# Second attention: high and low part of the values on 128 rows, two products per batch instead of three

## The reference

```python
q = rmsnorm(hidden @ Wq.T, q_norm_w)
k = rmsnorm(repeat(ctx @ Wk.T, 4), k_norm_w)
v = repeat(ctx @ Wv.T, 4)
scores = einsum('bhqd,bhkd->bhqk', q, k) / sqrt(128) + mask
probs = softmax(scores)
x = x + einsum('bhqk,bhkd->bqhd', probs, v).reshape(...) @ Wo.T
```

## Time and profile before

| what | value |
|---|---|
| median of 3 runs | 1542.92 us (1541.38 to 1546.04) |
| the profiled execution | 1540.48 us, its span 1538.7 us |
| mean granted TensorE clock | 0.990 of full speed |
| TensorE products, busy | 1498.0 us, 97% of the span, 9676 instructions |
| VectorE, busy | 1011.8 us, 66% |
| ScalarE, busy | 819.7 us, 53% |
| GpSimd, busy | 382.1 us, 25% |
| DMA | mean 39 GB/s |
| value products of the second attention (L905) | 384 instructions, 39.64 us busy |

### The profile page before, as it was taken

How to read it: one execution, slowest core, us unless ns; L and a number is a source line. 1 busy time by engine, 2 the same in 40 slices (tenths; PEclk the granted TensorE clock), 3 DMA queues, 4 the chain that set the end, 5 groups by cost and what they waited for, 6 DMA issues and landing times.

```text
span 1538.7 us, 27892 instructions
## 1 busy us (share of the span) xinstructions
PE 1498.0 (97%) x9676; PEld 1320.9 (86%) x9676; DVE 1011.8 (66%) x2475; ACT 819.7 (53%) x2862; POOL 382.1 (25%) x390
## 2 busy tenths in 40 slices
PE   8999999999999999999999999999999999889997
PEld 8999999999989998787888888888888887777785
DVE  7566556655665567875666666566666688788775
ACT  5456455645554555446565656555556563555542
POOL 5102010201021012133232323233232331543420
PEclk9999999999999999999999999999999999989998
DMA  6000100100010101110101010101010110111001
GB/s 220 29 28 28 42 29 28 42 28 28 28 56 1 42 29 29 53 42 28 42 28 42 29 42 28 42 28 42 29 53 18 36 56 8 38 36 62 28 8 58
DMA packets 14768, 60.22 MB, mean 39 GB/s; under 512 B 2100, under 2 KB 3508, under 8 KB 9640
## 3 DMA queue, kind: packets, MB, share of 16 engines
q1 hardware_dynamic: 14632, 58.46, 10.9%
HBM read 56.36 MB, written 2.10 MB: 38 GB/s over the span
## 4 chain that ended last, share of the span: by engine, by line
PE 59%; issue 27%; DVE 7%; POOL 4%; ACT 2%; DMA 0%; POOLq 0%; DVEq 0%; ACTq 0%
PE psY L918 15%; PE psQ L837 11%; PE psKV L859 8%; PE psSO L806 3%; PE psSO L905 2%; PE psTP L869 2%; PE psQ L822 2%; PE psSO L807 2%; POOL wo L513 1%; PE psTP L822 1%; PE psTP L889 1%; PE psKV L1251 1%; PE psQ L1205 1%; PE psQ L762 1%; PE psSO L1234 1%
## 5 line engine op out<-in xcount | busy, mean ns | idle before, releaser
L918 PE MATMUL psY<-wo,oT 128*128 128x512 f32 x1536 | 384.9, 399 | 0.9 <-POOL wo L513 0.2
L918 PEld LDWEIGHTS psY<-wo,oT 128*128 128x128 f32 x1536 | 278.2, 188 | 64.9 <-POOL wo L513 2.3
L513 POOL TENSOR_TENSOR wo<-stage_o,wo 128x512 fp32r<-128x512 f32 x68 | 87.3, 1316 | 310.4 <-ACT wo L1350 310.4
L1350 ACT ACTIVATE pT<-psTP 128x512 fp32r<-128x512 f32 (+1 forms) x128 | 62.8, 491 | 162.3 <-PE psTP L889 162.3
L1442 ACT ACTIVATE prob<-wide,neg_mx 128x128 f32<-128x128 f32 x256 | 99.7, 391 | 82.1 <-DVE neg_mx L1980 82.1
L628 POOL TENSOR_TENSOR rms<-ms_eps,minus_half 128x5 f32<-128x5 f32 (+1 forms) x64 | 74.2, 1159 | 259.5 <-DVE ms_eps L1997 258.7
L1439 ACT ACTIVATE prob<-s_sb,neg_mx 128x64 f32<-128x64 f32 x256 | 86.0, 337 | 95.1 <-DVE neg_mx L1980 95.1
L1825 DVE TENSOR_TENSOR pT<-psTP,pT 128x512 fp32r<-128x512 f32 (+1 forms) x128 | 71.2, 556 | 76.4 <-ACT pT L1350 75.7
L859 PEld LDWEIGHTS psKV<-wkv,arena 128*128 128x128 f32 x768 | 99.8, 190 | 9.1 <-DVE kT L2027 4.6
L859 PE MATMUL psKV<-wkv,arena 128*128 128x256 f32 x768 | 103.3, 284 | 1.5 <-DVE kT L2027 1.5
L837 PE MATMUL psQ<-wq,hT 128*128 128x512 f32 x384 | 103.9, 408 | 0.0
(11 more groups left out here) (334 smaller groups left out, 3451.0 us busy)
## 6 DMA issues: line engine op xcount, KB each, us to landing
stage_o<-in_wo SPq DMA_DIRECT2D x16, 1024.0 KB, 4.7
stage_q<-in_wq SPq DMA_DIRECT2D x15, 1024.0 KB, 5.3
stage_kv<-in_wkv SPq DMA_DIRECT2D x12, 512.0 KB, 3.8
stage_q<-in_ctx SPq DMA_DIRECT2D x16, 256.0 KB, 2.8
stage_o<-in_ctxT SPq DMA_DIRECT2D x2, 1024.0 KB, 5.0
stage_q<-in_base SPq DMA_DIRECT2D x2, 1024.0 KB, 4.9
out<-x_res SPq DMA_DIRECT2D x8, 256.0 KB, 2.3
stage_q<-in_wq SPq DMA_DIRECT2D x4, 256.0 KB, 4.9
```

Source lines behind the costliest of these rows:

```text
L513: g.tensor_tensor(dst[LO], stage, dst[HI].bitcast(f32), ALU.subtract).then_inc(ld[done or what + "_lo"], 1)
L918: m = mm(psY[:], oT[:, ol, h, :], wo[:, wl, h, :], start=h == 0 and i == 0, stop=h == HQ - 1 and i == 2)
L1350: copy = lambda o, i: nc.scalar.activation(o, i, ACT.Copy)
```

## The change

The two batches' operands are laid out so that each product contracts 128 rows. For batch 0, the tile of v has the high part in rows 0 to 63 and the low part in rows 64 to 127; for batch 1 the other way round. pT has, for each part and each batch, a block of 256 columns (`p_stack`): the high block of a batch holds the high part of its probabilities twice, once in each half of the rows, and the low block holds the low part in the batch's own rows and zeros in the other 64. A product with the high block gives high x high and low x high together, one with the low block gives high x low. That is two products for each batch.

ScalarE now writes the high part of pT in four copies of 64 rows, two of which move from one half of the partitions to the other, and v's high part in two; VectorE makes pT's low part in two instructions and v's in two, the latter across the halves. The zeros are written once, in the first expert layer's fourth step. The squares' junk goes to `wide`, as pT is now full, and SyncE's loads into `wide` wait for the last squares.

```diff
-    junk_q = [pT[:, h // 2, (2 + h % 2) * HD:(3 + h % 2) * HD] for h in range(HQ)]
+    junk_q = [wide[:, h * HD:(h + 1) * HD] for h in range(HQ)]
+    def rows_of(b):
+        return slice(b * S, (b + 1) * S)
+    def p_stack(b, hl):
+        return pT[:, hl, b * 256:(b + 1) * 256]
...
-        sp.wait_ge(A["exp"], STEPS)
+        sp.wait_ge(A["squares"], 2 * STEPS)
...
-                    for i, (vl, pl) in enumerate(PASSES):
+                    for pl in (HI, LO):
                         for b in range(2):
-                            rows = slice(b * S, (b + 1) * S)
-                            m = mm(psO[:, b, 0:256], a.v[rows, u.res(a.ring), vl, 0:HD], pT[rows, pl, 0:256],
-                                   start=i == 0, stop=i == 2)
+                            m = mm(psO[:, b, 0:256], a.v[:, u.res(a.ring), b], p_stack(b, pl),
+                                   start=pl == HI, stop=pl == LO)
...
-                    copy(a.v[:, st.res(a.ring), HI], psKV[:, HD:2 * HD]).then_inc(s["v_hi"], 1)
+                    copy(a.v[rows_of(0), st.res(a.ring), 0], psKV[rows_of(0), HD:2 * HD])
+                    copy(a.v[rows_of(1), st.res(a.ring), 1], psKV[rows_of(1), HD:2 * HD]).then_inc(s["v_hi"], 1)
...
+                if a.rms:
+                    for b in range(2):
+                        copy(p_stack(b, HI)[rows_of(1 - b)], psP[rows_of(b), 0:256])
+                    copy(p_stack(0, HI)[rows_of(0)], psP[rows_of(0), 0:256])
+                    copy(p_stack(1, HI)[rows_of(1)], psP[rows_of(1), 0:256]).then_inc(s["pT_hi"], 1)
+                    return
...
-                    sub_hi(a.v[:, st.res(a.ring), LO], psKV[:, HD:2 * HD], a.v[:, st.res(a.ring), HI]).then_inc(s["v_lo"], 1)
+                    sub_hi(a.v[rows_of(1), st.res(a.ring), 0], psKV[rows_of(0), HD:2 * HD], a.v[rows_of(0), st.res(a.ring), 0])
+                    sub_hi(a.v[rows_of(0), st.res(a.ring), 1], psKV[rows_of(1), HD:2 * HD],
+                           a.v[rows_of(1), st.res(a.ring), 1]).then_inc(s["v_lo"], 1)
...
+                if a.rms:
+                    sub_hi(p_stack(0, LO)[rows_of(0)], psP[rows_of(0), 0:256], p_stack(0, HI)[rows_of(0)])
+                    sub_hi(p_stack(1, LO)[rows_of(1)], psP[rows_of(1), 0:256],
+                           p_stack(1, HI)[rows_of(1)]).then_inc(s["pT_lo"], 1)
+                    return
...
             if f.index == 0 and t == 3:
                 ln_norm(next_ln, 0)
+                for b in range(2):
+                    empty = p_stack(b, LO)[rows_of(1 - b)]
+                    link(V.tensor_scalar(empty.rearrange("p (a c) -> p a c", a=2),
+                                         ones[rows_of(1 - b)].unsqueeze(1).to_broadcast([S, 2, P]), 0.0, None, ALU.mult))
```

## The result

| | before | after |
|---|---|---|
| median of 20 runs each | 1543.41 us | 1548.54 us |
| profiled execution's span | 1538.7 us | 1545.9 us |
| ratio after / before | | 1.0031, 95% interval 1.0023 to 1.0039 |

The forecast was 1535.2 us, its range 1530.5 to 1541.5. The kernel became 5.1 us slower at the median. The forecast was wrong in sign, and the time lies above the range.

A forecast was written before the change was run, and what follows sets the result against it. TensorE, busy 591.84 of 595.00 us, was taken as the bound. A gain of 10.15 us less 2.47 (1.27, 0.5 and 0.7) gave net 7.7, from the median of 1542.92 to 1535.2 us; range 1530.5 to 1541.5.

The forecast's parts named there:

- The gain: Value products, four instead of six: 0.175 us off an ordinary step, 0.08 with wo copies, 10.15 us in all.
- Together with ScalarE's 0.17 the chain is 0.46 us later: v's pieces before the mask: 0.17 us on ScalarE, 0.29 on VectorE, hidden by 0.99 us cover at q's transpose.
- an almost even race: ScalarE's oT copy against TensorE's output products: oT about 0.1 us later, with more than a microsecond to spare.
- A 256-column copy holds ScalarE 0.27 us; three more add 0.81: pT's high part on ScalarE: 4 x 0.27 = 1.08 us, hidden under 1.69 us of cover.
- cover near 1.4 us: pT's low part on VectorE: ends near 906.9, value products start at 908.37, so no wait.
- 0.7 in seven steps: Steps with wo copies: wait at the next q transpose, 0.1 us taken (0 to 0.2) in each of seven.
- steps of 9.12: Sign in the changed kernel's timeline: steps of 9.12 us, and about 9.40 where wo is split.
- The start: Start of the stage, once: waits for prob and q_sb grow by 0.46 and 0.81; loss 1.27 us, bounds 0.8 and 2.
- (a): Helpers late in five more steps of eight, which keep their old length: 6.1 us of gain lost, 1541.3 us; chance 0.18.
- (c): ScalarE's chain becomes the bound if a pT copy holds it 0.60 us or more; at 0.65, 1557 us; chance 0.06.
- (b): Gaps around TensorE's value products stay, three slots become four: +7.2 us plus 2.5, 1552.6 us; chance 0.06.
- (d): No gain: something else holds the step, TensorE waits it out, one-time losses stay; 1545.4 us; chance 0.06.

The follow-up runs named there:

- v whole: Changed kernel with v in one copy and one subtraction again, pT still in pieces, so the products have other operands; ratio to before 0.9957.
- products alone: Kernel before with four 128-row value products in place of the six, on the old operands; 1532.57 us against 1542.64, ratio 0.9935.
- Without moved rows: Changed kernel with four 64-row pT copies that all stay in their own half of the partitions; profile only, middle 55 steps 509.9 us.

## Why the prediction was wrong

**Right: the products.** The gain was put at 10.15 us and is 10.1 alone. A step is 0.19 shorter (0.175). It is split otherwise than told, and that the sum came out is partly luck: last score product to first output product went from 0.73 to 0.64, not 0.55, because the first of the four products took 0.20 us to the next and not 0.118; and the output products up to q's transpose went from 2.87 to 2.76, where no gain was forecast. That part lies in the first of them: behind the six 64-row products the second output product starts 0.34 us after the first, behind the four 0.23. The second one in each, before (first at 741.13) and after (first at 765.19):

```profile
741.47 0.39 PE L918 MATMUL psY<-wo,oT 128*128 128x512 f32 x1
...
765.42 0.40 PE L923 MATMUL psY<-wo,oT 128*128 128x512 f32 x1
```

**The steps that failed** are two. The dearer one put v's pieces at nothing: "Together with ScalarE's 0.17 the chain is 0.46 us later. The next one to be late is q's transpose", and then "Hidden." With v whole the middle is 503.8 us instead of 512.6, so v's pieces make 8.8 of the 10.2 us by which it is longer than with the products alone. The prediction asked which TensorE instruction waits for the chain, found q's transpose with 0.99 us of cover, and called oT "an almost even race". It didn't ask what is queued behind prob on GpSimd. The wkv step went 0.32 us over its old length by it, seven times. The race for oT was lost in every step: the copy starts 3.88 us behind the value products (777.62) with no wait for TensorE, where it had been 3.67, and with v whole it is 3.57. That costs only in the wo step, where kT's cover is gone: its kv products start 7.26 us behind the value products, with v whole 6.94.

The other one is "A 256-column copy holds ScalarE 0.27 us; three more add 0.81". The 0.27 was read where neighbours use the same rows. Between pieces in changing halves the next start waits for the end: 1.55 us instead of 1.08. And pT's low part was checked against the value products only in the ordinary step ("cover near 1.4 us"), not in the wo step, where the copies start 7.33 us behind the value products (781.07) and not 5.7: there the value products waited, 0.21 us. With v whole these 0.2 are all that is left of the four copies' price in the middle.

Both together made the follower late, by the prediction's own sum: its 0.42 us of the pT copies, with 0.47 more, and 0.57 of v are 1.46 against a cover of 0.99, an estimate of 0.47. Measured, q's transpose starts 3.76 us behind the value products there instead of 3.31, 0.45 later. Without moved rows the sum gives 0.23 and the trace 0.27; with v whole it stays under the cover, and the trace has 0.02. So the mechanism was right in this step and two terms too small. "0.7 in seven steps" became 0.35 + 0.30 over the old lengths, 4.6 us, where the forecast had 0.08 + 0.08 off them; the steps of 9.12 that it named as a sign came, those of 9.40 were 9.83.

**Sizes.** The chain before the mask grew by 0.57 us (0.46 taken). The zeros took 0.61 us on VectorE and 0.76 on the path (0.5 taken, bound 0.9):

```profile
650.50 0.61 DVE L2229 TENSOR_SCALAR pT<-ones 64x256 fp32r<-64x256 f32 x2
```

In the four kernels that write them two steps later that layer is back at 50.1 us. The start cost 2.85 us (1.27 taken, bound 2): the waits on prob and q_sb grew by 0.39 and 1.11 (0.46 and 0.81 taken), and behind them came two on pT that the prediction didn't have (0.19 at the first value products, 0.28 at the second), another of 0.29 on q_sb, and the slower projection, less the 1.08 us wait on kT that it swallowed. The last six steps lost 1.15 us, where a gain of about 0.8 was counted.

**The rivals.** The nearest is (a), helpers late in more steps, but it put them in the five steps with weight slices and had them only give up their gain. The late ones were three of eight, and instead of falling back to their old length they went past it by 0.32 us each. (c) gave 0.60 us a copy as the point of decision; the copy held 0.39, and in the wo step and its follower, which had less cover, that was enough. (b) and (d) fell with the products alone.

**Open.** Four copies in a row over all 128 rows have no run, nor have two moved ones in the same halves, so the reading of ScalarE's overlap rests on the orders of 64-row copies above. That the kernel with no moved rows keeps its wkv step at 9.63 follows from v, but of its total there is only the profiled execution. GpSimd's wkv splits ahead of their wait for prob weren't tried. When the clock falls at the start of the stage isn't known: with the same waits in front it fell in one kernel's execution and not in another's.

## What to carry to other kernels

Price an instruction cut into pieces by its start-to-start distance between neighbours of the same kind, partitions included, and not by that of the whole. A cover is as thin as it is in the thinnest step of the pattern: work through the step with the extra slices as carefully as the ordinary one, and follow each delayed result into every engine's queue, GpSimd's too. If a helper's chain is late at the start of a stage, filling TensorE's gap or keeping its clock buys little; the chain has to be cut.

## What the runs showed of the hardware

- ScalarE overlapped neighbouring 64-row copies (0.28 us from start to start for copies of 0.38) only where both read and wrote the same half of the partitions; in every order with a changed half it was 0.38 to 0.40 (a change of half and a moved copy aren't told apart where one half changes). A copy that moves rows across halves lasted no longer than one in place.
- Going from 64-row products to full-height ones, TensorE took 0.34 us from the first full-height product of 512 columns to the second, and 0.23 where no 64-row product stood in front.
- VectorE's copy within SBUF took 1.0 to 1.3 us each beside GpSimd's splits and 0.59 for two without them; its subtractions from PSUM didn't change.
- TensorE's clock fell to 1.2 GHz behind waits of 1.62 and 1.05 us, and in another kernel behind waits of 0.51 and 1.05, with which it stayed up in the kernel before; the twelve products then took 4.58 and 4.44 us instead of 2.99 and 3.01, and the stage was only 0.35 and 0.12 us longer.
